# A decoder layer on one core: instruction orders, engine choices and PSUM banks laid out anew

## The chip, the cores and the metric

The kernel runs on one core of one Trainium2 chip, in one launch. The metric is the device time of that core in microseconds (us). Three runs of the kernel before took 178.32, 179.06 and 180.08 us; the median is 179.06 us.

## The reference

The layer has three parts on `x` (16 sequences of 128 tokens, 256 channels), each followed by a residual and a layer norm:

```python
x = layernorm(x + attention(x))          # 16 heads of 16 channels, 4 key/value heads, RMS norm, rope, causal
x = layernorm(x + wkv(x, ctx))           # channelwise recurrence over the 128 tokens, keys x, values ctx
x = layernorm(x + ffn(x))                # 256 -> 1024 -> 256, weights are signs, relu, per-channel scales
```

Attention: `q`, `k`, `v` by one projection with biases, `q` and `k` divided by their root mean square, rotated, `q` times a gain, causal softmax, and an output projection with bias. `wkv`: numerator and denominator of a weighted mean decay by `exp(-exp(time_decay))` at every token; the current token has the weight `exp(time_first)`. The feed-forward part: `relu(x @ sign(up).T) * up_scale`, then `@ sign(down).T * down_scale * output_scale`.

## The kernel before

The 16 sequences are worked on in 8 pairs `p` (`T = 2` sequences `t` in each). Every engine has one instruction stream, and all of them are written out by hand: small functions (`project`, `scores`, `exps`, `normed`, `low_bits`, ...) issue the instructions of one step of one pair, and a long list of calls at the end of each engine's block sets the order. Up to some seven pairs are under way at once, in different steps. Engines wait for each other by semaphores, one per step (`done(engine, step, p)`). A table `ON` says for the steps that several engines can do which engine does it for each pair (`V` VectorE, `G` GpSimd, which the profile calls POOL, `A` ScalarE). The eight PSUM banks are handed out by tables too (`PJ`, `SC`, `PV`, `AC`, `WO`, `X1`, `YT`, `X2`, `DN`, `UP`).

The steps of a pair, with the names used later:

- **project** (L417, L423): TensorE multiplies x by the weights in float32, then adds the biases by a matmul of ones with `bias_rows` (three bf16 rows that sum to the float32 bias, made by `split` on VectorE, L1518 to L1524, from a load of the biases into 96 partitions).
- **squares, head_sums, mean_log, first_root, newton_rms**: the root mean square of each head on ScalarE (square, logarithm, exponential) and VectorE; **rope_sines, rope_cosines, rope_sum** on VectorE; **scale_heads** gives `qn`; **high_heads, low_heads** split it in two float16 parts (`stack`), **swap_keys** writes the keys a second time the other way round. SyncE transposes `stack` to `rows` by DMA; for pair 0 TensorE does it (**first_rows**, L431) and ScalarE and VectorE copy the result out (L964, L1628).
- **scores** (L472, L479), **exps** (L971), **products** (L500), **attention_to_tokens**, **attend_norm**, **attention_to_channels**, **project_out** (L533), **residual** (0, the sum r1).
- layer norm n (0, 1 or 2): **moments(n, p)** on VectorE (L1676), **inverse_root** and **root** on POOL (L1355, L1361), then **normed(n, p)**, on VectorE (L1691) in two instructions that take the mean and the factor, or on ScalarE (L1035), which needs **offsets(n, p)** (L1682) from VectorE first.
- the recurrence: **keys**, **keys_by_context**, **scan** (L1702, VectorE, one instruction over numerator and denominator), **mix** (L1712), then the quotient by **log_den, first_rec, den_by_rec** (L1729, or L1395 on POOL)**, num_by_rec** (L1734, or L1400 on POOL)**, refine, add_mixed**.
- the feed-forward part in four quarters n: **high_x2, low_x2**, **ffn_up** (L576), **relu** (L1019), **high_bits** (L1025, float16 part), **low_bits** (L1760, the rest), **ffn_down** (L597), **scale_out** (L1766), **add_out** (L1773), layer norm 2, **store** by SyncE.

The code holds a second version of the attention scores for large gains (`row_scores`, `row_maxima`), which subtracts row maxima first. A flag computed on the chip from the gains chooses. TensorE reads it once (L612) and has two whole bodies, plain and guarded. VectorE reads it once and has eight short conditional blocks around `row_maxima(p)`. With these inputs the plain path runs.

## Time and profile before

| | |
|---|---|
| runs | 178.32, 179.06, 180.08 us |
| profiled execution, first to last instruction | 178.1 us (no time of its own is listed beside this span) |
| TensorE matmuls | 157.8 us busy, 89% of the span |
| VectorE | 156.5 us, 88% |
| ScalarE | 138.9 us, 78% |
| POOL | 83.4 us, 47% |
| mean granted TensorE clock | 0.979 |

The trace is of one execution. Busy shares are means over a beginning in which one pair is under way, a long middle in which several are, and an end in which only the last pair is left. What bounds each of them is to be read from its own stretch: which engine has hardly any idle time there, and, in the idle time of an engine, what ended it (`<-` and the name of the instruction that released it).

### The profile page before, as it was taken

To read this page: it belongs to the slowest core of one execution; us is meant where nothing else is said; L and a number is where in the kernel's file an instruction comes from. 1 tells how busy PE (TensorE), PEld (TensorE's weight loads), DVE (VectorE), ACT (ScalarE), POOL (GpSimd) and SP (SyncE) were. 2 spreads that over 40 slices of the span, in tenths; PEclk is the share of its full clock that TensorE was granted. 3 is DMA by queue.
4 is the path that set the end of the run, shared out by engine and by line. 5 is a ranking of instruction groups with operands and counts; after the bars stand their busy time and mean duration, and the time that the engine had idled before them with its cause. 6 is when DMAs were issued, how large, how long until landed. Compare 5 with 4: busy or idle time off the path is not lost.

```text
span 178.1 us, 3837 instructions
## 1 busy us (share of the span) xinstructions
PE 157.8 (89%) x1388; PEld 107.8 (61%) x1388; DVE 156.5 (88%) x289; ACT 138.9 (78%) x280; POOL 83.4 (47%) x109
## 2 busy tenths in 40 slices
PE   7978769989999999999999999999969798999920
PEld 2445424545645645566886668769758687898810
DVE  1489679798789999999899999999999999999981
ACT  3745488988998889999899989696687897898700
POOL 8282601017404695020873623699679457270121
PEclk9999969999999999999999999999999999999995
DMA  5899039044709107941070310000300010001122
GB/s 175 244 320 392 5 62 209 2 92 75 249 0 95 56 2 94 212 127 48 0 151 0 75 48 2 0 4 0 118 0 4 0 59 0 36 27 61 63 79 107
DMA packets 17989, 14.65 MB, mean 82 GB/s; under 512 B 12656, under 2 KB 13616, under 8 KB 17712
## 3 DMA queue, kind: packets, MB, share of 16 engines
q1 hardware_dynamic: 17424, 13.87, 29.8%
q10 hardware_dynamic: 544, 0.50, 0.9%
q8 instruction: 13, 0.21, 0.5%
q14 instruction: 8, 0.07, 0.1%
HBM read 9.52 MB, written 2.10 MB: 65 GB/s over the span
## 4 chain that ended last, share of the span: by engine, by line
PE 48%; DVE 27%; ACT 10%; issue 8%; DMA 3%; POOL 2%; SPq 0%; POOLq 0%; DVEq 0%; ACTq 0%
PE banks L417 9%; PE banks L576 8%; PE banks L500 7%; PE banks L597 6%; PE banks L533 5%; DVE hid_lo L1760 5%; DVE state L1702 4%; PE banks L472 4%; ACT probs L971 3%; DMA probs<-biases_dram 3%; DVE ratio L1712 2%; DVE stats L1676 2%; PE banks L510 2%; ACT dn_sb L918 2%; PE banks L479 2%
## 5 line engine op out<-in xcount | busy, mean ns | idle before, releaser
L971 ACT ACTIVATE probs<-banks 128x1024 f32<-128x1024 f32 x32 | 31.8, 1022 | 4.8 <-PE banks L479 4.8
L597 PE MATMUL banks<-dn_sb,hid_hi 128*128 128x256 bf16 x128 | 29.1, 272 | 1.1 <-DVE hid_lo L1760 1.1
L576 PE MATMUL banks<-x2hi,up_sb 128*128 128x256 f16 x128 | 29.1, 273 | 0.8 <-DVE x2lo L1753 0.5
L597 PE MATMUL banks<-dn_sb,hid_lo 128*128 128x256 bf16 x128 | 29.1, 273 | 0.0
L576 PE MATMUL banks<-x2lo,up_sb 128*128 128x256 f16 x128 | 29.0, 272 | 0.0
L417 PE MATMUL banks<-wqkv_sb,xT_sb 128*128 128x384 f32 x64 | 23.5, 512 | 2.0 <-issue 1.6
L1355 POOL TENSOR_SCALAR veps<-stats 128x2 f32<-128x2 f32 x24 | 9.4, 394 | 27.8 <-DVE stats L1676 26.8
L1361 POOL TENSOR_TENSOR rstd<-veps,half_neg 128x2 f32<-128x2 f32 x24 | 20.4, 853 | 1.3
L1019 ACT ACTIVATE banks<-banks,ups_man 128x256 f32<-128x256 f32 x48 | 19.6, 470 | 1.8 <-PE banks L576 1.6
L417 PEld LDWEIGHTS banks<-wqkv_sb,xT_sb 128*128 128x128 f32 x64 | 12.4, 201 | 11.9 <-issue 3.4
L1702 DVE TENSOR_TENSOR_SCAN state<-dec_sb,ke 128x1032 f32<-128x1032 f32 x8 | 18.4, 2301 | 0.0
L500 PE MATMUL banks<-probs,v_sb 128*32 128x512 f32 x128 | 17.6, 632 | 0.2
L576 PEld LDWEIGHTS banks<-x2hi,up_sb 128*128 128x128 f16 x128 | 12.5, 98 | 6.0 <-issue 3.8
L1760 DVE TENSOR_TENSOR hid_lo<-banks,hid_hi 128x512 f16<-128x512 f32 x24 | 16.0, 679 | 0.0
L1025 ACT ACTIVATE hid_hi<-banks 128x512 f16<-128x512 f32 x24 | 14.3, 616 | 1.7 <-PE banks L597 0.8
L533 PE MATMUL banks<-wo_sb,attT_sb 128*128 128x256 f32 x64 | 15.1, 379 | 0.0
L597 PEld LDWEIGHTS banks<-dn_sb,hid_hi 128*128 128x128 f16 x128 | 12.5, 98 | 3.4 <-issue 1.8
L597 PEld LDWEIGHTS banks<-dn_sb,hid_lo 128*128 128x128 f16 x128 | 12.5, 98 | 1.5
L576 PEld LDWEIGHTS banks<-x2lo,up_sb 128*128 128x128 f16 x128 | 12.5, 98 | 1.4
L533 PEld LDWEIGHTS banks<-wo_sb,attT_sb 128*128 128x128 f32 x64 | 12.2, 190 | 1.5
L472 PE MATMUL banks<-rows 32*128 32x512 f16 x128 | 10.2, 394 | 3.2 <-ACT probs L971 1.5
L1405 POOL TENSOR_TENSOR hid_lo<-hid,hid_hi 128x512 f16<-128x512 f32 x5 | 5.8, 1168 | 14.7 <-ACT hid_hi L1025 14.6
(129 smaller groups left out, 355.8 us busy)
## 6 DMA issues: line engine op xcount, KB each, us to landing
ctxT_sb<-ctxT_dram SPq DMA_DIRECT2D x8, 256.0 KB, 3.1
x_sb<-x_dram SPq DMA_DIRECT2D x8, 256.0 KB, 3.8
out_dram<-outb SPq DMA_DIRECT2D x8, 256.0 KB, 2.2
xT_sb<-xT_dram SPq DMA_DIRECT2D x7, 256.0 KB, 4.4
up_f<-up_dram SPq DMA_DIRECT2D x1, 1024.0 KB, 6.4
dn_f<-down_dram SPq DMA_DIRECT2D x1, 1024.0 KB, 8.4
wqkv_sb<-wqkv_dram ACTq DMA_DIRECT2D x2, 192.0 KB, 3.1
xT_sb<-xT_dram SPq DMA_DIRECT2D x2, 128.0 KB, 2.9
```

The source lines that it names most:

```text
L417: nc.tensor.matmul(banks[:, b + t, 0:E], xT_sb[:, p % XT_N, c, t, :], wqkv_sb[:, c, :], start=(c == 0), stop=False)
L472: nc.tensor.matmul(banks[:, b[g]], q[r:r + VW, kb, :], q[r:r + VW, HB * t:HB * t + REP, :].rearrange("p j s -> p (j s)"), start=(k == 0), ...
L500: nc.tensor.matmul(banks[r:r + VW, PV[p][t], :], v_sb[:, p % V_N, t, g, :], probs[:, (T * p + t) % PROBS_N, g].rearrange("p j s -> p (j s) ...
L533: mm = nc.tensor.matmul(banks[:, WO[p], t * D:(t + 1) * D], attT_sb[:, c, t, :], wo_sb[:, c, :], start=False, stop=(t == T - 1 and c == NC ...
L576: mm = nc.tensor.matmul(banks[:, UP[p][n], s * T * S:(s + 1) * T * S], up_sb[:, c, j * 128:(j + 1) * 128], part[:, c, :, :].rearrange("p t ...
L597: mm = nc.tensor.matmul(banks[:, DN[p], t * D:(t + 1) * D], part[:, t * S:(t + 1) * S], down_of(j), start=(j == 0 and t == 0 and m == 0), ...
L971: nc.scalar.activation(probs[:, (T * p + t) % PROBS_N, 2 * h:2 * h + 2].rearrange("p n j s -> p n (j s)"), banks[:, b:b + 2], ACT.Exp).the ...
L1019: nc.scalar.activation(hidden(p, n)[:, s], banks[:, UP[p][n], s * T * S:(s + 1) * T * S], ACT.Relu, scale=ups_man[:, j:j + 1]).then_inc(se ...
L1025: nc.scalar.activation(hid_hi[:, 2 * n:2 * n + 2], hidden(p, n), ACT.Copy)\
L1361: nc.gpsimd.tensor_tensor(rstd[n][:, p % MV_N], veps[n][:, p % MV_N], half_neg[:], ALU.pow)\
L1702: nc.vector.tensor_tensor_scan(state[:, 1:2 * W + 1], dec_sb[:].rearrange("p c a t s -> p (c a t s)"), ke[:, p % KE_N].rearrange("p c a t ...
L1760: nc.vector.tensor_tensor(hid_lo[:, 2 * n:2 * n + 2], hidden(p, n), hid_hi[:, 2 * n:2 * n + 2], ALU.subtract).then_inc(signal(f"lo{n}_done ...
```

## The change

What it does:

1. The lists of calls on all five engines are in another order, and the tables of banks hold other numbers.
2. `ON` has other engines: `low_heads` is always on POOL (before three of eight on VectorE), `swap_keys` four times on VectorE (before once), seven of 32 `high_bits` on POOL (before none), and more of the recurrence's products on POOL. `hid` in SBUF or PSUM is chosen by a table `HID`.
3. More norms on ScalarE: before `normed(1, p)` of all pairs; now `normed(0, p)` for pairs 5 and 6, `normed(1, p)` for 0 to 6 and `normed(2, p)` for 0, 1, 2, 5 and 6 (`NORM_ON_ACT`), with `offsets` on VectorE for each of them.
4. VectorE has one branch: after the flag there are two whole bodies, as on TensorE. TensorE reads the flag after `project(3)` and `first_rows`, no longer after `project(1)`.
5. The biases are loaded into three partitions (0, 32, 64) in one DMA, into a buffer (`outb`) that VectorE clears first; before, they went into 96 partitions in two DMAs. The output bias is split on VectorE, before on POOL. The load of the gains moves from ScalarE's queue to SyncE's.
6. The last pair's end is divided by sequence: the last quarter of `ffn_down(7)` by halves, `scale_half` and `add_half` instead of `scale_out` and `add_out`, and two stores of half the size.

TensorE, from `project(1)` to the first scores (xT_sb: the tokens by channel; flags: the branch). Before:

```order
L417 MATMUL banks<-wqkv_sb,xT_sb 128x384 x4
L423 MATMUL banks<-bias_rows,ones_b 128x384 x2
L612 TENSOR_LOAD flags
L612 ISA x2
L869 COMPARE_AND_BRANCH
L417 MATMUL banks<-wqkv_sb,xT_sb 128x384 x4
L423 MATMUL banks<-bias_rows,ones_b 128x384 x2
L417 MATMUL banks<-wqkv_sb,xT_sb 128x384 x4
L423 MATMUL banks<-bias_rows,ones_b 128x384 x2
L431 MATMUL banks<-id_h,stack 128x128 x12
L472 MATMUL banks<-rows 128x512 x8
```

Now:

```order
L434 MATMUL banks<-wqkv_sb,xT_sb 128x384 x4
L440 MATMUL banks<-bias_rows,ones_b 128x384 x2
L434 MATMUL banks<-wqkv_sb,xT_sb 128x384 x4
L440 MATMUL banks<-bias_rows,ones_b 128x384 x2
L434 MATMUL banks<-wqkv_sb,xT_sb 128x384 x4
L440 MATMUL banks<-bias_rows,ones_b 128x384 x2
L448 MATMUL banks<-id_h,stack 128x128 x12
L648 TENSOR_LOAD flags
L648 ISA x2
L883 COMPARE_AND_BRANCH
L495 MATMUL banks<-rows 128x512 x8
```

Two projections and the transposition of pair 0 stand ahead of the read of the flag, which stands right ahead of the first scores.

VectorE's last instructions (r: the sum before norm 2; outb: what is stored). Before:

```order
L1760 TENSOR_TENSOR hid_lo<-banks,hid_hi 128x512
L1691 TENSOR_SCALAR outb<-r,stats,rstd 128x256 x2
L1676 BN_STATS stats<-r 128x6
L1766 TENSOR_TENSOR banks<-banks,dsc_b 128x512
L1773 TENSOR_TENSOR r<-banks,x 128x512
L1691 TENSOR_SCALAR outb<-r,stats,rstd 128x256 x2
L1676 BN_STATS stats<-r 128x6
L1691 TENSOR_SCALAR outb<-r,stats,rstd 128x256 x2
```

Now:

```order
L1751 TENSOR_TENSOR hid_lo<-banks,hid_hi 128x512
L1757 TENSOR_TENSOR r<-banks,dsc_b 128x512
L1670 SCALAR_TENSOR_TENSOR offset<-stats,rstd 128x2
L1751 TENSOR_TENSOR hid_lo<-banks,hid_hi 128x512
L1664 BN_STATS stats<-r 128x6
L1770 TENSOR_TENSOR banks<-banks,dsc_b 128x256
L1775 TENSOR_TENSOR r<-banks,x 128x256
L1770 TENSOR_TENSOR banks<-banks,dsc_b 128x256
L1775 TENSOR_TENSOR r<-banks,x 128x256
L1664 BN_STATS stats<-r 128x6
L1670 SCALAR_TENSOR_TENSOR offset<-stats,rstd 128x2
L1679 TENSOR_SCALAR outb<-r,stats,rstd 128x256 x2
```

The scaling and the addition of the last pair are four instructions of half the size, and `normed(2, 6)`, which stood between the addition and the last moments, is gone to ScalarE (its offset is left, after the last moments).

POOL, from `keys_by_context(6)` on. Before:

```order
L1389 TENSOR_TENSOR ke<-ke,ctxT_sb 128x2x2x128
L1355 TENSOR_SCALAR veps1<-stats1 128x2
L1361 TENSOR_TENSOR rstd1<-veps1,half_neg 128x2
L1389 TENSOR_TENSOR ke<-ke,ctxT_sb 128x2x2x128
L1400 TENSOR_TENSOR ratio<-ratio,rec0 128x2x256
L1405 TENSOR_TENSOR hid_lo<-hid,hid_hi 128x512
L1411 TENSOR_TENSOR r3<-r3,x2 128x512
L1355 TENSOR_SCALAR veps1<-stats1 128x2
L1361 TENSOR_TENSOR rstd1<-veps1,half_neg 128x2
```

Now:

```order
L1371 TENSOR_TENSOR ke<-ke,ctxT_sb 128x2x2x128 x2
L1343 TENSOR_TENSOR rstd2<-veps2,half_neg 128x2
L1382 TENSOR_TENSOR ratio<-ratio,rec0 128x2x256
L1377 TENSOR_TENSOR newt<-ratio,rec0 128x512
L1392 TENSOR_TENSOR hid_lo<-hid,hid_hi 128x512
L1387 CAST hid_hi<-hid 128x512
L1337 TENSOR_SCALAR veps1<-stats1 128x2
L1343 TENSOR_TENSOR rstd1<-veps1,half_neg 128x2
L1387 CAST hid_hi<-hid 128x512
L1392 TENSOR_TENSOR hid_lo<-hid,hid_hi 128x512
```

The addition is gone from here to VectorE, and both products of pair 6 and three parts `hid_hi` of later pairs have come or moved up.

The diff, cut (function bodies that only change names, and the lists of calls, are left out but for a few lines):

```diff
         ON = dict(
-            qn_done="GGVVGGGV",
-            hi_done="AGGGGAGA",
-            lo_done="VGVVGGGG",
-            stack_done="AVAAAAAA",
-            kv_done="VGVVGVGG",
-            newt_done="GGGVGGVG",
-            guess_done="VVVGGVGV",
-            lo2_done="GGGVGGVV",
-            r3_done="GGVGVVVV")
+            guess_done="GVVGGVGV",
+            hi0_done="GGAGAGAA",
+            hi2_done="AGAAAGGA",
+            hi_done="AGAGGGAA",
+            kv_done="VGGVGVGG",
+            lo1_done="VVGVVVVV",
+            lo2_done="GVVVVVVV",
+            lo3_done="VVGVGGVV",
+            newt_done="GGGGGGGV",
+            out_done="AAAVVAAV",
+            qn_done="VGVGVGGV",
+            r3_done="GVVVVVGV",
+            stack_done="AAVVVAVA",
+            x1_done="VVVVVAAV",
+            x2_done="AAAAAAAV")
+        NORM_ON_ACT = ((0, 0, 0, 0, 0, 1, 1, 0), (1, 1, 1, 1, 1, 1, 1, 0), (1, 1, 1, 0, 0, 1, 1, 0))
...
-            sp.dma_start(bias_in[:, 0:E], biases[0:E].partition_broadcast(BR)).then_inc(bias_in_done, 16)
+            sp.wait_ge(bias_clear, 1)
+            sp.dma_start(bias_in[0:BR:32], biases.partition_broadcast(3)).then_inc(bias_in_done, 16)
+            for dst, src in gain_loads:
+                sp.dma_start(dst, src).then_inc(gains_in, 16)
...
-            store(7)
+            store_half(7, 0)
+            store_half(7, 1)
...
             project(0)
             project(1)
-            pe.wait_ge(masks_ready, MASKS)
-            pe.wait_ge(guard_ready, GUARDS)
+            project(2)
+            done(pe, "rot_done", 0)
+            project(3)
+            first_rows()
             pe.wait_ge(gain_ready, GAINS)
             plain = pe.value_load(flags[0:1, 0:1], min_val=0, max_val=1)
...
+            def ffn_down_half(p, t):
+                n = NJ // 2 - 1
+                hidden_there(p, n)
+                for s in range(2):
+                    j = 2 * n + s
+                    for m, part in enumerate((hid_hi, hid_lo)):
+                        mm = nc.tensor.matmul(down_tile(p, t), part[:, j, t * S:(t + 1) * S], dn_sb[:, j],
+                                              start=False, stop=(s == 1 and m == 1))
+                mm.then_inc(sems["dn_mm"], 1)
...
+            def high_bits(p, n):
+                done(pool, "hid_done", p, 2 * n + 2)
+                nc.gpsimd.tensor_copy(hid_hi[:, 2 * n:2 * n + 2], hidden(p, n)).then_inc(signal(f"hi{n}_done", p), 1)
...
+            nc.vector.memset(bias_in, 0.0).then_inc(bias_clear, 1)
...
-            with dve.If(guarded):
-                row_maxima(0)
...
+            def scale_half(p, t):
+                done(dve, "dn_mm", p, NJ // 2 + t)
+                nc.vector.tensor_tensor(down_tile(p, t), down_tile(p, t), dsc_b[:], ALU.mult).then_inc(sems["o3_done"], 1)
+            def add_half(p, t):
+                done(dve, "o3_done", p, t + 1)
+                nc.vector.tensor_tensor(r3[:, p % R3_N, t], down_tile(p, t), x2[:, p % X2_N, t], ALU.add)\
+                    .then_inc(signal("r3_done", p), 1)
...
+            with dve.If(plain):
+                from_heads(False)
+            with dve.Else():
+                from_heads(True)
```

## Rows read from the trace of the kernel before

**Rows 1.** The page, part 1: busy us (share of the span), xinstructions.
```profile
PE 157.8 (89%) x1388; PEld 107.8 (61%) x1388; DVE 156.5 (88%) x289; ACT 138.9 (78%) x280; POOL 83.4 (47%) x109
```

**Rows 2.** Windows: us, busy PE, PEld, DVE, ACT, POOL (x); granted clock, DMA share, GB/s.
```profile
110.00:150.00 40.00, 36.38 (x319) 29.94 (x317) 39.84 (x65) 31.63 (x68) 28.34 (x28) 1.00 0.06 20
160.00:170.00 10.00, 10.00 (x94) 8.81 (x93) 9.13 (x18) 7.69 (x17) 1.17 (x3) 1.00 0.15 56
```

**Rows 3.** Timeline from 0 to 22 us: start us, busy us, engine, line, operation, idle before.
```profile
4.68 3.88 PE L417 MATMUL banks<-wqkv_sb,xT_sb 128*128 128x384 f32 x8
...
8.92 0.50 PE L423 MATMUL banks<-bias_rows,ones_b 96*128 96x384 bf16 x2 [0.35 <-DVE bias_rows L1524]
...
12.20 0.61 POOL L1338 CAST maskq_sb<-probs 128x512 bf16<-128x512 f32 x1
...
13.92 2.84 PE L417 MATMUL banks<-wqkv_sb,xT_sb 128*128 128x384 f32 x8 [1.59 <-issue]
...
17.88 0.51 ACT L957 ACTIVATE stack<-stack 128x128 f16<-128x128 f16 x2
...
19.83 0.83 PE L431 MATMUL banks<-id_h,stack 128*128 128x128 f16 x12
...
21.78 0.40 PE L472 MATMUL banks<-rows 32*128 32x512 f16 x4 [1.12 <-ACT rows L964]
```

**Rows 4.** Timeline from 22 to 26 us, VectorE and TensorE.
```profile
22.30 0.83 DVE L1612 TENSOR_TENSOR banks<-banks,cos_sb 128x640 f32<-128x640 f32 x1 [0.45 <-issue]
...
24.10 1.04 PE L472 MATMUL banks<-rows 32*128 32x512 f16 x8 [1.48 <-ACT probs L971]
```

**Rows 5.** Windows of 24 to 27 us and of 29 to 31 us.
```profile
24.00:27.00 3.00, 2.90 (x32) 0.93 (x32) 1.98 (x6) 2.23 (x5) 0.00 (x0) 0.51 0.94 97
29.00:31.00 2.00, 2.00 (x19) 0.85 (x21) 1.91 (x7) 1.35 (x3) 0.72 (x1) 1.00 0.79 288
```

**Rows 6.** Groups by line and shape: xcount | busy us, mean ns | idle before.
```profile
L1035 ACT ACTIVATE x<-z,offset,rstd 128x256 f32<-128x256 f32 x16 | 8.8, 613 | 1.3 <-DVE offset L1682 1.2
L1395 POOL TENSOR_TENSOR newt<-ratio,rec 128x512 f32<-128x512 f32 x6 | 7.6, 1268 | 7.9 <-ACT rec L1004 7.8
...
L1381 POOL TENSOR_TENSOR stack<-qn,stack 128x640 f16<-128x640 f32 x5 | 7.0, 1402 | 0.4 <-ACT stack L948 0.2
...
L1691 DVE TENSOR_SCALAR outb<-r,stats,rstd 128x256 f32<-128x256 f32 x16 | 5.8, 404 | 1.2 <-POOL rstd L1361 1.2
...
L1642 DVE TENSOR_TENSOR stack<-qn,stack 128x640 f16<-128x640 f32 x3 | 2.5, 822 | 0.2
...
L1682 DVE SCALAR_TENSOR_TENSOR offset<-stats,rstd 128x2 f32<-128x2 f32 x8 | 1.5, 190 | 0.0
...
L1338 POOL CAST maskq_sb<-probs 128x512 bf16<-128x512 f32 x1 | 0.6, 613 | 0.1
```

**Rows 7.** Timeline from 138 to 144 us: a scan on VectorE and a product on POOL.
```profile
139.83 2.29 DVE L1702 TENSOR_TENSOR_SCAN state<-dec_sb,ke 128x1032 f32<-128x1032 f32 x1
...
140.71 2.48 POOL L1400 TENSOR_TENSOR ratio<-ratio,rec 128x512 f32<-128x512 f32 x1 [2.74 <-ACT rec L1004]
```

**Rows 8.** Timeline of the end, from 170 us, VectorE and POOL.
```profile
170.49 0.70 DVE L1766 TENSOR_TENSOR banks<-banks,dsc_b 128x512 f32<-128x512 f32 x1
...
172.54 0.69 DVE L1676 BATCH_NORM_STATS2 stats<-r 128x6 f32<-128x512 f32 x1
...
173.67 0.69 POOL L1361 TENSOR_TENSOR rstd<-veps,half_neg 128x2 f32<-128x2 f32 x1
174.47 0.73 DVE L1691 TENSOR_SCALAR outb<-r,stats,rstd 128x256 f32<-128x256 f32 x2 [1.23 <-POOL rstd L1361]
```

**Rows 9.** Waits of SyncE's queue: us in total, times, longest us.
```profile
SPq L284 <- DMA out_dram<-outb: 2.1, 1, 2.1
```

**Rows 10.** DMA issues: tile, queue, count, KB each, median us from issue to landing.
```profile
xT_sb<-xT_dram SPq DMA_DIRECT2D x2, 128.0 KB, 2.9
...
probs<-biases_dram SPq DMA_DIRECT2D x1, 144.0 KB, 5.3
```

More of the change, by code:

```diff
@@ L614, in from_scores @@
             def from_scores(guarded):
-                project(2)
-                done(pe, "rot_done", 0)
-                project(3)
-                done(pe, "rot_done", 1)
-                first_rows()
                 if guarded:
@@ L1752, in low_x2 @@
                 done(dve, "x2hi_done", p)
[L1753 to L1755 removed]
+                if X2_BY_DMA[p]:
+                    high, low = [x2h[:, p % X2H_N, part].rearrange("p t c d -> p (t c d)") for part in range(2)]
+                    whole = x2[:, p % X2_N].rearrange("p t d -> p (t d)")
+                else:
+                    high, low, whole = x2_part(p, 0), x2_part(p, 1), banks[:, X2[p]]
+                nc.vector.tensor_tensor(low, whole, high, ALU.subtract).then_inc(signal("x2lo_done", p), 1)
             def low_bits(p, n):
@@ L1827, in _ @@
-            done(dve, "rscale_done", 4)
-            head_sums(5)
-            rope_sines(5)
-            attend_norm(1)
-            rope_cosines(5)
-            normed(0, 0)
-            rope_sum(5)
-            newton_rms(5)
-            keys_by_context(0)
-            scan(0)
-            residual(1)
-            mix(0)
-            with dve.If(guarded):
-                row_maxima(3)
-            moments(0, 1)
-            rope_sines(6)
-            rope_cosines(6)
-            attend_norm(2)
@@ L1863, in _ @@
-            offsets(1, 0)
-            rope_cosines(7)
-            rope_sum(7)
-            scan(1)
-            with dve.If(guarded):
-                row_maxima(5)
-            residual(3)
-            mix(1)
-            low_x2(0)
-            newton_rms(7)
-            keys_by_context(2)
-            attend_norm(4)
-            moments(0, 3)
-            num_by_rec(1)
-            scale_heads(7)
-            scan(2)
-            refine(1)
-            low_bits(0, 0)
-            done(dve, "ny_done", 1)
@@ L1901, in _ @@
-            done(dve, "x1_done", 3)
-            residual(5)
-            with dve.If(guarded):
-                row_maxima(7)
-            low_x2(1)
-            keys_by_context(3)
-            offsets(1, 2)
-            scan(3)
-            moments(0, 5)
-            moments(2, 0)
-            mix(3)
-            low_bits(1, 0)
-            done(dve, "ratio_done", 3)
-            scan(4)
-            low_x2(2)
-            attend_norm(6)
-            low_bits(1, 1)
-            den_by_rec(3)
```

1074 lines of the change are left out of this document (548 added, 526 removed).

## The prediction

> **What bounds the kernel now.** I read the page's busy line first, then the windows, then the two ends in the timeline. The busy line [rows 1] has TensorE and VectorE nearly level at 89 and 88% of 178.1 us, so no single engine is the bound, and the stretches must say it. The windows [rows 2] say it: from 110 to 150 us VectorE is busy for 39.8 of 40 us, while TensorE is idle for 3.6 us of them, ScalarE for 8.4 and POOL for 11.7. From 160 to 170 us the order is turned round: TensorE is full, VectorE has 9.13. So the middle waits for VectorE, and the last pairs for TensorE.
>
> The beginning is a chain of short waits, each of which the reader finds in the bracket of a row. TensorE's first projection runs from 4.68 to 8.56 us, and its bias matmul waits for the bias rows until 8.92, a wait of 0.35 [rows 3]. After project(1) TensorE stands for 1.59 us, "issue": it has the table of masks to wait for, whose last cast on POOL ends at 12.81 (12.20 + 0.61), and then reads the flag and branches, another 1.1 us until 13.92 [rows 3]. Pair 0's heads are ready in `stack` at 18.39 (17.88 + 0.51), but TensorE only comes to them behind project(3), at 19.83. It then waits 1.12 us for ScalarE's copy of the rows, and the first scores start at 21.78. The next scores wait 1.48 us and start at 24.10 [rows 4], and from 24 to 27 us the granted clock is 0.51, the lower of TensorE's two levels, 1.2 GHz [rows 5].
>
> The end is one chain on VectorE and POOL after TensorE's last matmul: the scale starts at 170.49, then come the addition and a norm of pair 6, the moments at 172.54, the root on POOL at 173.67, the norm from 174.47 to 175.20 [rows 8], and then the store, for which SyncE waits 2.1 us [rows 9].
>
> **The beginning: -2.0 us.** The load of the biases (144 KB in 96 rows) takes 5.3 us to land; the first tokens, issued just before, take 2.9 [rows 10]. Three rows in place of 96 land between these two, sooner by up to 2.4 us, or not at all sooner if they queue behind the same traffic. It hardly matters: project(0) itself ends at 8.56, so at most 0.35 us comes of it [rows 3]. The clearing of the buffer is a memset on an idle VectorE while SyncE issues the tokens, cost nothing; if SyncE had to wait for it, the slack of the bias covers some tenths. The load of the gains, moved in front of the rope tables and all later loads on SyncE, delays these by one issue, under half a microsecond, and none was waited for.
>
> TensorE then runs projects 1, 2 and 3 without a stop. Project(1) ended 1.59 us ahead of 13.92, at 12.33, and now ends at 12.0; projects 2 and 3 took from 13.92 to 19.83, so project(3) ends at 12.0 + 5.9 = 17.9 [rows 3]. The stack of pair 0 must be ready by then. In the new order its scaling is on VectorE (0.8 instead of 1.3 us, by the nearest rows), its low part on POOL (1.40 instead of 0.82, [rows 6]); the two cancel, and what is left are ScalarE's earlier start by 0.35 and a key swap with less ahead of it, which puts the stack at about 17.6 to 18.0. So first_rows starts at 17.9 against 19.83, 2.0 us earlier. The read of the flag now stands behind it: 1.1 us, and it lies beside ScalarE's copy of the rows, in which TensorE stood for 1.12 us anyway [rows 3]; without that cover it would cost its 1.1. The first scores start at 19.7 and the second at about 22.1, where the rotation of pair 2 on VectorE and the first exponentials come out together. The fall of the clock has the same two waits ahead of it, so I leave it in. On TensorE the same work lies between there and project(5) in both orders. Bounds: 0.35 us (the stack is late and nothing moves) and 2.0 + 1.5, when the clock doesn't fall (3 us at half speed, [rows 5]).
>
> **One branch on VectorE: 0.** The eight conditional blocks look costly and are not: the first, with the read of the flag, leaves 0.45 us of issue [rows 4], and of the two microseconds from 29 to 31 us, in which the second one stands, VectorE is busy for 1.91 [rows 5]. The read now stands ahead of head_sums(0), where VectorE has to wait for the first squares. There are 0 to 0.5 + 7 x 0.09 = 1.1 us to have, if every idle time is the branch's; VectorE did not bound that part, so I take 0.
>
> VectorE must now jump over the guarded body at its end. The row that bears on it is SyncE's wait of 2.1 us for the last store [rows 9], which starts as VectorE is done and covers a jump of up to that length; the sum has 0 for it. The Trainium skill, "Runtime: NRT & Kernel Launch", section "Instruction fetch mechanics", speaks against this change: a taken branch to a target outside the fetched window forces a fetch before execution goes on. By that rule the end would still be hidden as long as the fetch is shorter than the store, and no row here shows VectorE making such a jump.
>
> **The middle: -2.0 us.** VectorE's work falls. Norms: 12 halves less at 0.404 (-4.8), low heads three less at 0.82 (-2.5), offsets six more at 0.19 (+1.1) [rows 6]. The other moves are products and additions of 0.7 to 0.8 us, three away and two come, key swaps, and the output bias with four small instructions: together about +1.7. The sum is -4.5 of 156.5 us. From 110 to 150 us alone it is ten halves less (norm 0 of pairs 5 and 6, norm 2 of pairs 0, 1 and 2), -4.0, and five offsets, +0.95; two products leave and two additions come. That is -3.1 us where VectorE has no idle time. It can pay out only until TensorE is full, and TensorE's idle time there is 3.6 us. ScalarE gets twelve halves more, at 0.613 each 7.4 us in all, and gives back seven `hid_hi` and six short copies [rows 6]; it has the 8.4 us of idle time in this stretch to take them. I take 2.0 of the 3.1, since each norm on ScalarE adds an offset and a turn in another queue to its chain, and POOL's products are slower. Bounds: 0, and 3.6.
>
> POOL gets three low heads at 1.40, seven casts of 128x512 at 0.6 (the nearest is the mask's, [rows 6]) and three products at about 1.3, and gives away some. That is +7 us on an engine with 53% idle time, so in sum free, but not in latency. The row to see is POOL's product at 140.71: it takes 2.48 us, where its like takes 1.27, because VectorE's scan runs from 139.83 to 142.12 [rows 6, 7]. The Trainium skill, "SBUF — State Buffer", section "Who interferes with whom", says that a VectorE instruction with two SBUF inputs and a GpSimd instruction that reads SBUF lock each other out for a whole instruction. The row agrees: the product ends 1.07 us after the scan. By the rule each of the 13 added POOL instructions may be stretched so; this is the third rival below.
>
> **The end: -0.9 us.** Scaling the first sequence starts under TensorE's last matmuls. After the last one, half a scale and half an addition are left, about 0.8 if each half of a 0.70 costs 0.4, and the norm of pair 6 is gone. So the moments start 0.8 to 0.9 us after the last matmul and not 172.54 - 170.49 = 2.05 [rows 8]: -1.2. Against it, the last store is two issues, the second issued about 0.4 later than one alone would be (a norm half is 0.404, [rows 6], and the first issue takes about as long): +0.3. Bounds: 0, if the halves cost as much as wholes, and -1.3.
>
> **Sum.** -2.0 - 2.0 - 0.9 = -4.9, with nothing between 30 and 110 us, where both engines are nearly full. 178.1 - 4.9 = 173.2 us of span. The median of the runs is 0.9 us above this execution's span, so I forecast a median of 174.1, 2.8% less.
>
> **Rivals.**
> - *The middle gives nothing* (17%): the chain from VectorE to POOL to ScalarE and back is as long as the work taken off VectorE. For it: ScalarE waited for an offset already in the trace (1.2 us in [rows 6]). Against: the full VectorE windows. 174.1 + 2.0 = 176.1.
> - *More than that* (12%): the clock doesn't fall at 24 us, or TensorE's idle time in the middle vanishes. 174.1 - 1.6 = 172.5. For it: the beginning has one stop of 1.6 us less. Against: the two waits right ahead of the fall stay [rows 3, 4].
> - *Slower* (9%): POOL's longer list is held up by VectorE's scans and products, on the way to the heads and to ffn_down, which waits for `hid_hi` and then `hid_lo`. Each hold costs 1.2 us (2.48 less 1.27, [rows 6, 7]). All 13 added instructions on the path would cost 15.6, half of them 7.8: 174.1 + 7.8 = 181.9. It turns the gain of 4.9 when more than four of the 13 are on the path. Against it: POOL is idle for 11.7 of the 40 us in which the lists are longest [rows 2].
> - *No change* (12%): four such holds, or the order of one engine wrong in one place (a load behind a wait on SyncE's queue: ctx of pair 6 now stands behind store(0), before ahead of it). 179.
> - The forecast's own case has 50%, from 172.8 to 175.5.
>
> A difference of 1% (1.8 us) is what a measurement can tell from no change. Faster by over 1% are the forecast, the first two rivals and little else: 0.78. Within 1%: 0.13. Slower: 0.09. The range of 8 in 10 leaves out the slower case and the outer tail of the best: 171.5 to 177.8.
>
> **What would show it.** First scores near 19.7 us and first_rows near 17.9; no issue gap after project(1); a gap of about 1.1 us ahead of the first scores. TensorE busy for over 38 of the 40 us in the middle, ScalarE for over 36. A fall of the granted clock near 22 us, as before at 24. From TensorE's last matmul to the last moments' start 0.9 us. It is wrong if POOL's casts take over 1 us each, if TensorE waits for `hid_hi` on POOL, or if VectorE's windows stay at 9.9 with the same end: then the work was put elsewhere on it.

## The result, and the profile after

The changed kernel takes 182.60 us (median of four runs, 182.25 to 183.03), the kernel before, measured beside it, 178.69 (177.56 to 180.08): a ratio of 1.0205, 95% interval 1.0146 to 1.0264. It is slower by 3.9 us; 174.1 was forecast.

The busy line of the page after, against [rows 1]:

```profile
PE 156.7 (87%) x1388; PEld 107.3 (59%) x1388; DVE 161.2 (89%) x291; ACT 141.4 (78%) x280; POOL 91.4 (51%) x115
```

VectorE was to fall from 156.5 to 152.0 us and rose to 161.2. The timeline of the beginning (start, busy, engine, line) answers to [rows 3, 4], and the window to [rows 5]:

```profile
17.37 0.84 PE L448 MATMUL banks<-id_h,stack 128*128 128x128 f16 x12
...
19.33 0.61 PE L495 MATMUL banks<-rows 32*128 32x512 f16 x8 [1.12 <-ACT rows L975]
...
22.08 0.61 PE L495 MATMUL banks<-rows 32*128 32x512 f16 x8 [1.92 <-DVE rot L1614]
```

```profile
24.00:27.00 3.00, 3.00 (x20) 1.29 (x22) 2.96 (x6) 2.52 (x7) 0.00 (x0) 1.00 0.85 189
```

The beginning came as forecast and a little better: first_rows starts 2.5 us sooner and the first scores at 19.33 (19.7 forecast). The fall of the clock at 24 us, which the forecast left in, is gone: the granted clock is 1.00 from 24 to 27 us, where it was 0.51. The first matmul of scores(1) starts at 27.80, before at 30.50. Then the lead is lost. From there to the first matmul of ffn_up(1) it is 66.8 us before and 71.0 now, and from that one to the last instruction 80.8 before and 81.75 now. In the middle [rows 2], TensorE's idle time fell as hoped, from 3.6 to 2.4 us of 40, and VectorE is as full as it was:

```profile
110.00:120.00 10.00, 9.39 (x92) 7.46 (x89) 9.97 (x17) 7.54 (x15) 4.81 (x6) 1.00 0.01 2
120.00:130.00 10.00, 9.88 (x80) 7.68 (x79) 9.97 (x18) 8.67 (x19) 6.94 (x9) 1.00 0.00 0
130.00:140.00 10.00, 9.09 (x79) 7.41 (x76) 9.91 (x18) 9.67 (x24) 7.71 (x11) 1.00 0.22 80
140.00:150.00 10.00, 9.27 (x84) 8.19 (x85) 9.97 (x16) 9.57 (x23) 5.20 (x6) 1.00 0.07 27
```

Where VectorE's time went shows when groups are kept apart by shape (count | busy us, mean ns | idle before):

```profile
L1751 DVE TENSOR_TENSOR hid_lo<-banks,hid_hi 128x512 f16<-128x512 f32 x19 | 12.6, 680 | 0.1
L1679 DVE TENSOR_SCALAR x<-r,stats,rstd 128x256 f32<-128x256 f32 x12 | 7.5, 668 | 0.0
L1751 DVE TENSOR_TENSOR hid_lo<-hid,hid_hi 128x512 f16<-128x512 f32 x8 | 7.0, 870 | 0.1
L1630 DVE TENSOR_TENSOR qn<-rot,rscale 128x640 f32<-128x640 f32 x4 | 4.2, 1061 | 0.1
```

A norm half takes 404 ns in [rows 6] and 668 here on average; a subtraction from SBUF 870, the same one from PSUM 680; a scaling of the heads 1061 where 820 is usual. Most instructions of a group have their usual length and a few are 0.3 to 1.2 us longer. VectorE and POOL in the timeline show when:

```profile
27.32 0.20 DVE L1585 TENSOR_TENSOR rscale<-ny,gain_b 128x40 f32<-128x40 f32 x1
...
27.60 1.28 POOL L1350 TENSOR_TENSOR qn<-rot,rscale 128x640 f32<-128x640 f32 x1 [5.47 <-DVE rscale L1585]
27.65 1.38 DVE L1550 TENSOR_SCALAR dsc_b<-dsc_b,osc_b 128x256 f32<-128x256 f32 x1
28.95 0.72 POOL L1356 CAST stack<-qn 128x640 f16<-128x640 f32 x1
29.06 0.62 DVE L1552 TENSOR_SCALAR u_rest<-u_clip 128x2 f32<-128x2 f32 x1
29.62 1.40 POOL L1363 TENSOR_TENSOR stack<-qn,stack 128x640 f16<-128x640 f32 x1
29.72 1.33 DVE L1554 TENSOR_SCALAR k_bias<-u_rest 128x2 f32<-128x2 f32 x1
...
62.51 0.69 POOL L1343 TENSOR_TENSOR rstd<-veps,half_neg 128x2 f32<-128x2 f32 x1
63.02 1.82 DVE L1679 TENSOR_SCALAR x<-r,stats,rstd 128x256 f32<-128x256 f32 x2
63.16 1.53 POOL L1363 TENSOR_TENSOR stack<-qn,stack 128x640 f16<-128x640 f32 x1
```

An instruction on two elements per partition (`k_bias`, 128x2) takes 1.33 us: it started 0.10 us after a POOL instruction and ended with it, at 31.05 and 31.02. The two norm halves at 63.02 take 1.82 us in place of 0.72 and end at 64.84, POOL's `low_heads` at 64.69. Laid beside POOL's, 14 of VectorE's instructions in this trace are too long by 10.6 us in all, each overlapping a POOL instruction that reads SBUF. In the trace before there are four, 2.3 us. No reduction, no batch statistics and no instruction with an operand in PSUM is among them, though such instructions often start inside a POOL read too: 35 products, sums and differences with a PSUM operand do so in the trace after, and none of them is longer by over 0.03 us. An instruction that is too long in this way is called held below, and the time too much a hold.

### The profile page after: what moved, and what is told of

Read it like the earlier page. It is cut to its first block, busy times and chain, and to the rows that moved or that the text cites. A ratio compares the mean times of both kernels' runs of the same rounds, so it can differ in the third digit from the quotient of the medians.

```text
span 180.5 us, 3809 instructions
## 1 busy us (share of the span) xinstructions
PE 156.7 (87%) x1388; PEld 107.3 (59%) x1388; DVE 161.2 (89%) x291; ACT 141.4 (78%) x280; POOL 91.4 (51%) x115
## 4 chain that ended last, share of the span: by engine, by line
DVE 55%; PE 19%; issue 11%; ACT 10%; POOL 2%; POOLq 0%; DVEq 0%; ACTq 0%
DVE state L1690 9%; DVE hid_lo L1751 6%; PE banks L434 5%; DVE stats L1664 5%; DVE ratio L1700 4%; PE banks L600 4%; ACT probs L982 3%; DVE banks L1607 3%; DVE rope_b L1600 3%; DVE rot L1614 3%; PE banks L621 2%; DVE ssum L1570 2%; DVE x2T L1746 2%; DVE z L1735 2%; PE banks L639 2%
## 5 line engine op out<-in xcount | busy, mean ns | idle before, releaser
L600 PE MATMUL banks<-x2T,up_sb 128*128 128x256 f16 x256 | 32.3, 273 | 1.8 <-DVE x2T L1746 1.7
L621 PE MATMUL banks<-dn_sb,hid_hi 128*128 128x256 bf16 x124 | 28.5, 273 | 0.8 <-DVE hid_lo L1751 0.6
L621 PE MATMUL banks<-dn_sb,hid_lo 128*128 128x256 bf16 x124 | 28.5, 273 | 0.0
L600 PEld LDWEIGHTS banks<-x2T,up_sb 128*128 128x128 f16 x256 | 24.3, 98 | 6.8 <-DVE x2T L1746 3.0
L1343 POOL TENSOR_TENSOR rstd<-veps,half_neg 128x2 f32<-128x2 f32 x24 | 18.2, 758 | 1.5
L1035 ACT ACTIVATE banks<-banks,ups_man 128x256 f32<-128x256 f32 x38 | 15.7, 461 | 3.8 <-PE banks L600 3.7
L523 PE MATMUL banks<-probs,v_sb 128*32 128x512 f32 x128 | 16.6, 603 | 0.0
L1363 POOL TENSOR_TENSOR stack<-qn,stack 128x640 f16<-128x640 f32 x8 | 11.7, 1472 | 8.2 <-ACT stack L959 8.1
L1751 DVE TENSOR_TENSOR hid_lo<-banks,hid_hi 128x512 f16<-128x512 f32 x19 | 12.6, 680 | 0.1
L1700 DVE SCALAR_TENSOR_TENSOR ratio<-ke,now_gain,state 128x512 f32<-128x512 f32 x16 | 12.7, 832 | 0.0
L1377 POOL TENSOR_TENSOR newt<-ratio,rec 128x512 f32<-128x512 f32 x7 | 10.2, 1451 | 3.8 <-ACT rec L1015 3.7
L1664 DVE BATCH_NORM_STATS2 stats<-r 128x6 f32<-128x512 f32 x16 | 11.1, 697 | 0.9 <-POOL r L1398 0.7
```

The source lines that it names most:

```text
L523: nc.tensor.matmul(banks[r:r + VW, PV[p][t], :], v_sb[:, p % V_N, t, g, :], probs[:, (T * p + t) % PROBS_N, g].rearrange("p j s -> p (j s) ...
L600: mm = nc.tensor.matmul(banks[:, UP[p][n], s * T * S:(s + 1) * T * S] .rearrange("p (t s) -> p t s", t=T), up_sb[:, c, j * 128:(j + 1) * 1 ...
L621: mm = nc.tensor.matmul(down_tile(p, t), part[:, j, t * S:(t + 1) * S], dn_sb[:, j], start=(j == 0 and m == 0 and (t == 0 or p == PAIRS - 1)),
L1035: nc.scalar.activation(hidden(p, n)[:, s], banks[:, UP[p][n], s * T * S:(s + 1) * T * S], ACT.Relu, scale=ups_man[:, j:j + 1]).then_inc(se ...
L1343: nc.gpsimd.tensor_tensor(rstd[n][:, p % MV_N], veps[n][:, p % MV_N], half_neg[:], ALU.pow)\
L1664: nc.vector.bn_stats(stats[n][:, p % MV_N].rearrange("p t k -> p (t k)"), rows_of.rearrange("p t d -> p d t"))\
```

## The experiments

**Theory 1, the holds:** a VectorE instruction that starts inside a POOL instruction reading SBUF waits until that one ends. **Theory 2, the order:** the new lists and POOL's longer latency cost the time, and the stretched instructions lie in slack. Each ratio is to the runs of the kernel before in the same batch (their medians 178.8 to 179.2); differences between two changed kernels are differences of their medians.

### Holds taken out of the changed kernel

`e1_const` moves one call on VectorE, in both bodies:

```diff
+                small_constants()
                 rope_sines(3)
                 newton_rms(2)
...
                 newton_rms(3)
-                small_constants()
```

> The changed kernel with one edit: VectorE's six small constants stand ahead of rope_sines(3), where POOL has nothing to do, and not behind newton_rms(3), which releases POOL's scale_heads(3). Theory (a VectorE instruction that starts inside a POOL instruction that reads SBUF waits until that one ends): the three constants that took 1.38, 0.62 and 1.33 us take 0.35, 0.17 and 0.17, VectorE's busy time falls by about 2.6 us, head_sums(4) starts near 28.5 instead of 30.96, and the whole is 1.0 to 2.5 us faster than the changed kernel (about 180 to 181.5 where that has 182.6). Rival 1 (the time was lost in the order of the lists and in POOL's latency, the stretched constants lie in slack): the constants are short, but the whole stays within 0.5 us of the changed kernel. Rival 2 (the constants are slow in themselves): they stay at 1.4, 0.6 and 1.3.

180.96 us, ratio to before 1.0106 [1.0023, 1.0189]: 1.6 us faster than the change. The intervals of the two ratios overlap, the runs do not (180.63 to 181.48 here, 182.25 to 183.03 there). The same two constants in its timeline:

```profile
21.66 0.35 DVE L1550 TENSOR_SCALAR dsc_b<-dsc_b,osc_b 128x256 f32<-128x256 f32 x1
...
22.25 0.17 DVE L1554 TENSOR_SCALAR k_bias<-u_rest 128x2 f32<-128x2 f32 x1
```

They aren't slow in themselves (rival 2 falls), and they weren't in slack (rival 1 falls). head_sums(4) starts at 29.53, not 28.5: it waits for ScalarE's squares, so part of the 2.6 us met the next wait.

`e2_waits` adds waits on POOL and nothing else:

```diff
+            done(pool, "x1_done", 1)
             low_heads(5)
...
+            done(pool, "x1_done", 2)
             low_heads(6)
...
+            done(pool, "x1_done", 4)
             add_out(0)
```

> The changed kernel with three waits added on POOL and nothing else: low_heads(5) waits until VectorE's normed(0, 1) is done, low_heads(6) until normed(0, 2) is, add_out(0) until normed(0, 4) is. Theory (VectorE held by POOL's reads): the three norm halves of 1.50, 1.50 and 1.36 us become 0.40 each, VectorE's busy time falls by 3.1 us and the whole by 1.5 to 3, though POOL only gets more to wait for. Rival (POOL's latency is what costs): the whole stays, or becomes 0.5 to 2 us slower, since POOL's three instructions start up to 0.7 us later.

180.51 us, 1.0115 [1.0082, 1.0148]: 2.1 us faster, by waiting more. POOL starts after the norm, which is short again:

```profile
61.97 0.69 POOL L1343 TENSOR_TENSOR rstd<-veps,half_neg 128x2 f32<-128x2 f32 x1
62.48 0.73 DVE L1682 TENSOR_SCALAR x<-r,stats,rstd 128x256 f32<-128x256 f32 x2
63.29 1.41 POOL L1363 TENSOR_TENSOR stack<-qn,stack 128x640 f16<-128x640 f32 x1 [0.63 <-DVE x L1682]
```

By theory 2 more waiting on POOL could only have cost time. `e5_fix` has both edits and three more: two waits on POOL, and den_by_rec(1) goes from POOL to VectorE:

```diff
-            newt_done="GGGGGGGV",
+            newt_done="GVGGGGGV",
...
+            done(pool, "qn_done", 7)
             low_bits(0, 2)
...
+            done(pool, "ratio_done", 4)
             low_bits(2, 1)
```

> The changed kernel with the edits of e1_const and e2_waits together and three more: on POOL low_bits(0, 2) waits for VectorE's scale_heads(7) and low_bits(2, 1) for mix(4), and den_by_rec(1) is on VectorE. Theory (the time was lost to VectorE instructions that POOL's reads hold up, and the losses add): VectorE's busy time falls from 161.2 to about 153.5 us, the stretched norms, scale_heads(7) and mix(4) are gone, and the whole is near 177.7 us (176.5 to 179), below the kernel before. Rival (only what is lost ahead of 70 us counts, from then on TensorE or ScalarE bound it): near 180, as e2_waits.

178.46 us, 0.9968 [0.9928, 1.0009]: 4.1 us of the change's time are gone, the losses add. VectorE is busy for 155.2 us; 3.3 of them are holds that are left (a copy at 40 us, a mix at 82, four more from 96 to 105). Without them it would be 151.9. The other direction, VectorE holding POOL, stayed as it was: those of POOL's instructions that take over 0.25 us more than usual are too long by 10.1 us in all in the kernel before, 11.1 in the change and 11.0 in `e5_fix`.

`e6_writes` puts memsets, which read nothing, in the place of POOL's large products, sums, differences and casts. What these steps compute is left out; order and waits stay. For example in `low_bits`:

```diff
-                nc.gpsimd.tensor_tensor(hid_lo[:, 2 * n:2 * n + 2], hidden(p, n),
-                                        hid_hi[:, 2 * n:2 * n + 2], ALU.subtract).then_inc(signal(f"lo{n}_done", p), 1)
+                nc.gpsimd.memset(hid_lo[:, 2 * n:2 * n + 2], 0.0).then_inc(waste, 1)
+                wasted()
+                nc.gpsimd.memset(hid_lo[:, 2 * n:2 * n + 2], 0.0).then_inc(signal(f"lo{n}_done", p), 1)
```

> The changed kernel with all of POOL's products, sums, splits and casts of 128x512 and 128x640 replaced by memsets of their outputs, two or three in a row so that POOL is busy for about as long (1.0 to 1.4 us each); what these steps compute is left out, order, waits and semaphores stay. Theory (POOL's reading of SBUF holds VectorE, writing alone does not): no VectorE instruction is stretched any more, its busy time falls from 161.2 to about 151 us, and the whole is 173 to 177 us. Rival 1 (POOL's mere activity or its latency costs the time): stretches and the whole stay, 180 or more. Rival 2 (other things bind once VectorE is free): no stretches, yet 178 or more.

177.26 us, 0.9913 [0.9873, 0.9954]: 5.3 us less than the change, a little outside the range expected. The groups again:

```profile
L1703 DVE TENSOR_SCALAR x<-r,stats,rstd 128x256 f32<-128x256 f32 x12 | 6.9, 616 | 0.0
L1775 DVE TENSOR_TENSOR hid_lo<-hid,hid_hi 128x512 f16<-128x512 f32 x8 | 5.4, 679 | 0.1
L1654 DVE TENSOR_TENSOR qn<-rot,rscale 128x640 f32<-128x640 f32 x4 | 3.3, 820 | 0.1
```

Products and differences are at their normal 679 and 820 ns. The norms are not (616): beside memsets six halves took 0.69 to 0.95 us, and so did four of the small constants by `tensor_scalar` (0.39 to 0.75). So VectorE was busy for 155.1 us, not for the 151 expected. "Writing does not hold VectorE" was too wide: it holds the norm, not the product of two operands.

### Holds put into the kernel before

Those runs moved POOL's timing too. `e13_reads` adds seven products to `e3_head` (below) in POOL's idle time; `e14_memsets` has three memsets in the place of each:

```diff
+            def extra(name, p, k=None):
+                done(pool, name, p, k)
...
+                nc.gpsimd.tensor_tensor(scratch[:], up_f[:, 0, 0:512], up_f[:, 1, 0:512], ALU.mult).then_inc(waste, 1)
...
             keys_by_context(1)
+            extra("r1_done", 3)
             den_by_rec(1)
+            extra("guess_done", 1)
+            extra("scan_done", 2)
             low_bits(0, 2)
```

> The kernel of e3_head with seven extra products on POOL, two SBUF operands of 128x512 each, into a scratch buffer, at seven places where POOL is idle for at least 1.5 us and VectorE works without a pause (after residual(3), num_by_rec(1), scan(2), den_by_rec(3), low_bits(2, 0), the first mix(6) and num_by_rec(7)). None of POOL's own instructions has to start later. Theory (POOL's reads hold VectorE): four to seven VectorE instructions are stretched by 0.4 to 1.2 us, VectorE's busy time rises by 4 to 7 us, and the whole is 2 to 5 us slower than e3_head's 176.6. Rival (the holds only happened where VectorE had slack, or come from POOL's real work): the whole within 0.7 us of e3_head.

> As e13_reads, but each of the seven extra products is three memsets of the scratch buffer, about 1.3 us of POOL in all, which read nothing. Theory (it is the reading): no VectorE instruction with two SBUF operands is stretched, norms in halves by 0.4 us at most, and the whole is within 0.7 us of e3_head. Rival (any POOL instruction holds VectorE): as slow as e13_reads.

184.40 us, 1.0341 [1.0298, 1.0384], with reads; 177.18 us, 0.9936 [0.9904, 0.9969], with memsets. The first place, with reads:

```profile
70.71 2.42 DVE L1730 SCALAR_TENSOR_TENSOR ratio<-ke,now_gain,state 128x512 f32<-128x512 f32 x2
70.88 1.71 POOL L1422 TENSOR_TENSOR scratch<-up_f 128x512 f32<-128x512 f32 x1 [3.22 <-DVE r L1687]
```

with memsets:

```profile
70.89 1.41 DVE L1731 SCALAR_TENSOR_TENSOR ratio<-ke,now_gain,state 128x512 f32<-128x512 f32 x2
71.04 1.48 POOL L1423 MEMSET scratch<- 128x512 f32 x3 [3.21 <-DVE r L1688]
```

and the busy lines, reads first:

```profile
PE 158.8 (87%) x1388; PEld 108.5 (59%) x1388; DVE 164.5 (90%) x289; ACT 139.1 (76%) x280; POOL 94.2 (52%) x116
```

```profile
PE 156.0 (89%) x1388; PEld 107.3 (61%) x1388; DVE 156.6 (90%) x289; ACT 138.8 (79%) x280; POOL 92.4 (53%) x130
```

Seven products raise VectorE's busy time by 7.9 us and the whole by 7.2 against memsets in the same places. Two thirds of it are direct: six VectorE instructions overlap one of the products and are held by 5.7 us in all. Three more are held for 2.8 us by POOL's own reads, which by the delay come to lie beside other instructions than with memsets. The granted clock is 0.83 from 140 to 150 us in the profile with reads and 1.00 with memsets, but it carries little: two of the four executions with reads have mean clocks of 0.984 and 0.985, as high as with memsets, and are as slow as the others. This shows the cause without any call of the layer in another place, and a price: what VectorE lost in the full stretches, the kernel lost nearly one for one. In `e5_fix` it was less, 4.1 us for 6.0 of VectorE's. The first place shows both directions: the first half of `mix` holds the product (1.71 in place of 1.27), then the product holds the second half. The Trainium skill, "SBUF — State Buffer", section "Who interferes with whom", states this: whoever issues first has the shared ports for its whole instruction, and the other fully blocks; a VectorE instruction with two SBUF inputs contends with a GpSimd instruction that reads SBUF and not with one that only writes, and copies, casts and `tensor_scalar` can enter modes that contend with GpSimd. The traces agree: the two halves of mix took 2.42 us beside a read and 1.41 beside memsets, norms are longer beside reads (1.50 in the change) and beside memsets (up to 0.95 in `e6_writes`), PSUM operands and reductions beside neither.

### The other parts

`e3_head`, the kernel before with TensorE's new beginning alone:

```diff
             project(1)
+            project(2)
+            done(pe, "rot_done", 0)
+            project(3)
+            done(pe, "rot_done", 1)
+            first_rows()
             pe.wait_ge(masks_ready, MASKS)
```

> The kernel before with the changed kernel's beginning on TensorE alone: project(2), project(3) and first_rows stand ahead of the read of the flag and its waits. Theory (this term of the prediction was right, -2.0 us): first_rows starts near 18.3 and the first scores near 20.3 instead of 21.78, and the whole is 1 to 2 us faster than before. Rival: the next wait, for the rotation of pair 2 on VectorE or for the exponentials, takes the place, and the whole moves by less than 0.5 us.

176.62 us, 0.9874 [0.9793, 0.9954]: 2.35 us faster. About 0.9 of it may be the clock's. The granted clock is 1.00 from 24 to 27 us here, and against those ten of the batch's 19 executions of the kernel before whose mean clock is 0.987 or more (median 178.0), the gain is 1.4 us.

```profile
17.12 0.83 PE L431 MATMUL banks<-id_h,stack 128*128 128x128 f16 x12
19.11 0.61 PE L472 MATMUL banks<-rows 32*128 32x512 f16 x8 [1.16 <-DVE rows L1628]
```

`e8_low` adds to it three `low_heads` on POOL:

```diff
-            lo_done="VGVVGGGG",
+            lo_done="GGGGGGGG",
```

> The kernel of e3_head with low_heads of pairs 0, 2 and 3 on POOL, as the change has them (three instructions of 0.82 us off VectorE, 1.40 us each on POOL). By the prediction this gives VectorE 2.5 us, of which the whole keeps 0 to 1 (175.6 to 176.6). By the theory that POOL's reads hold VectorE, each of the three may stretch one VectorE instruction by up to 1.2 us, and with the longer chain to the first scores the whole is 0 to 2 us slower (176.6 to 178.6).

177.62 us, 0.9952 [0.9901, 1.0002]: 1.0 us slower than `e3_head`, though 2.5 us of VectorE's work are gone. The rows of pair 0 come later (first scores at 19.86, `e3_head` 19.11), and four instructions of VectorE are held that were not: three small ones by 0.3, 0.4 and 0.8 us, and the constant `dsc_b`, which starts with a `low_heads` at 27.54, by 1.2. That is 2.7 us, as much as was taken off.

`e7_norms` puts five norms of the middle on ScalarE in `e3_head`, `e12_outnorms` only the three whose result is stored; per norm:

```diff
-            normed(2, 0)            (VectorE's list)
+            offsets(2, 0)
...
+            normed(2, 0)            (ScalarE's list)
```

> The kernel of e3_head (before, with the new beginning) with five more layer norms on ScalarE, as the change has them in the middle: normed(0, 5), normed(0, 6), normed(2, 0), normed(2, 1), normed(2, 2), with offsets on VectorE in their places. The prediction's middle term: VectorE has 4.0 us less in halves and 0.95 more in offsets, and the whole falls by up to 2 us from e3_head's 176.6 (174.6 to 175.6). Rival (a norm by ScalarE lengthens its chain, and ScalarE is full where it is put): no change, or up to 2 us slower.

> The kernel of e3_head with only the norms whose result is just stored on ScalarE: normed(2, 0), normed(2, 1), normed(2, 2). e7_norms, with normed(0, 5) and normed(0, 6) as well, was 5.6 us slower than e3_head. If it is the turn VectorE, ScalarE, TensorE on the path of x1 that costs, this one is near e3_head (176 to 177.5); if every added norm on ScalarE holds up its queue, it is 2 to 4 us slower (178.6 to 180.6).

182.23 us, 1.0171 [1.0074, 1.0267], and 179.27 us, 1.0014 [0.9963, 1.0064]: 5.6 and 2.65 us slower than `e3_head`. In `e7_norms` VectorE is no longer full from 110 to 150 us (34.9 us of 40, `e3_head` 39.6), TensorE even less (33.8, `e3_head` 36.1), and ScalarE's waits name the turn (us in total, times, longest):

```profile
ACT x L1040 <- DVE offset L1693: 3.9, 3, 2.0
```

`e7_norms` came out slower than either expectation. `e12_outnorms` lies where it was expected if every added norm on ScalarE holds up its queue, and leaves 3.0 us for the two norms on the path of x1: both paths cost. But one must not read it as the term's sign. `e10_normback` does the reverse in `e5_fix`: the five norms are back on VectorE, their calls moved from ScalarE's list to VectorE's, and the tables say so:

```diff
-        NORM_ON_ACT = ((0, 0, 0, 0, 0, 1, 1, 0), (1, 1, 1, 1, 1, 1, 1, 0), (1, 1, 1, 0, 0, 1, 1, 0))
+        NORM_ON_ACT = ((0, 0, 0, 0, 0, 0, 0, 0), (1, 1, 1, 1, 1, 1, 1, 0), (0, 0, 0, 0, 0, 1, 1, 0))
```

> The kernel of e5_fix with the five norms of the middle back on VectorE: normed(0, 5), normed(0, 6), normed(2, 0), normed(2, 1), normed(2, 2). By the prediction's middle term they give VectorE 3 us of work where it is full, and the whole is 1.5 to 2.5 us slower than e5_fix's 178.5 (180 to 181). Rival (what VectorE was relieved of came back as waits for offsets and for ScalarE): within 0.7 us of e5_fix, or faster.

185.19 us, 1.0319 [1.0230, 1.0408]: 6.7 us slower than `e5_fix`, over three times what was expected. VectorE is busy for 5.0 us more, and 2.1 of them are three new holds (norm halves at 125 and 147 us, a mix at 148). TensorE stops more, and the granted clock falls behind it, where `e5_fix` has 1.00 from 110 to 150 us:

```profile
120.00:130.00 10.00, 7.64 (x58) 6.24 (x56) 9.97 (x19) 5.51 (x12) 5.71 (x8) 1.00 0.23 79
130.00:140.00 10.00, 9.73 (x73) 8.21 (x72) 8.85 (x14) 8.38 (x20) 6.42 (x8) 0.83 0.01 2
```

Either order of calls is slower with the other's engines for these five norms. So neither run prices the norms by themselves; it is order and engines together that the change moved.

The end. `e4_end` gives the kernel before the halves, with normed(2, 6) behind the last moments:

```diff
-            scale_out(7)
+            scale_half(7, 0)
             done(dve, "out_done", 5)
-            add_out(7)
+            add_half(7, 0)
+            scale_half(7, 1)
+            add_half(7, 1)
+            moments(2, 7)
             landed(dve, "stored", 4)
             normed(2, 6)
-            moments(2, 7)
```

> The kernel before with the changed kernel's end alone: the last quarter of ffn_down(7), the scale and the addition by sequence, two stores of half the size, and normed(2, 6) behind moments(2, 7) instead of ahead of it. Theory (this term was right, -0.9 us): the last moments start about 0.9 us after TensorE's last matmul instead of 2.05 after the start of the scale, and the whole is 0.7 to 1.4 us faster than before. Rival: the halves cost as much as wholes and the second store adds a latency; the whole stays within 0.3 us.

179.28 us, 1.0019 [0.9966, 1.0071]: nothing that the runs can show. VectorE comes to the first half late, and four halves take nearly as long as two wholes and a norm (1.78 us to the moments, 2.05 in [rows 8]):

```profile
169.45 0.27 PE L622 MATMUL banks<-dn_sb,hid_lo 128*128 128x256 bf16 x1
169.72 0.42 DVE L1803 TENSOR_TENSOR banks<-banks,dsc_b 128x256 f32<-128x256 f32 x1
...
171.50 0.70 DVE L1700 BATCH_NORM_STATS2 stats<-r 128x6 f32<-128x512 f32 x1
```

The first half starts as TensorE's last matmul ends, not under it. `e11_addout` takes away, in `e5_fix`, VectorE's wait for POOL's add_out(6): VectorE does the addition itself (`r3_done="GVVVVVVV"`):

> The kernel of e5_fix with add_out(6) on VectorE, not on POOL. In the changed kernel VectorE waits 0.72 us for it, right ahead of the last pair's halves. Theory (this wait ate most of the end's gain): the last moments start 0.6 to 0.7 us earlier against the last matmul, and the whole is 0.3 to 0.7 us faster than e5_fix (near 178.0). Rival (VectorE gets 0.6 us more work, which takes the wait's place): no change.

178.68 us, 1.0003 [0.9962, 1.0044]: no change, and the last moments start 1.78 us after the last matmul (`e5_fix` 1.86); the rival was right. `e9_best` is `e3_head` with the halves, normed(2, 5) and normed(2, 6) on ScalarE and a wait on POOL at two holds, as in `e2_waits`; `e15_end2` leaves these two waits out.

> The kernel of e3_head with two holds taken off VectorE (POOL's den_by_rec(0) waits for num_by_rec(0), POOL's add_out(0) for normed(0, 4)), the end by halves of e4_end, and normed(2, 5) and normed(2, 6) on ScalarE, which is idle there. Theory: 1.05 and 0.8 us of VectorE's time come back ahead of 95 us, and the last moments start about 0.9 us earlier against the last matmul than in e3_head; 174.5 to 175.8 us where e3_head has 176.6. Rival (VectorE's time does not bind there, the halves give nothing as in e4_end): 176.6.

> The kernel of e9_best without its two waits on POOL: the new beginning and the end by halves with normed(2, 5) and normed(2, 6) on ScalarE. In e9_best the last moments started 1.40 us after the end of TensorE's last matmul, in e3_head 2.10, yet its time was the same. If the two waits cost what the end gave, this is 0.5 to 0.8 us faster than e3_head (175.8 to 176.1); if not, it is 176.5.

176.48 us, 0.9853 [0.9782, 0.9923], and 176.98 us, 0.9906 [0.9876, 0.9936]. The last moments start 1.40 us after the last matmul in place of 2.10, and the whole does not show it against `e3_head`. Both holds were only exchanged: den_by_rec(0), made to wait, then held newton_rms by 0.98 us, and a keys_by_context held an offset at 66.4 us by 0.94. VectorE's holds are 2.2 us in all, as in `e3_head`. These two and `e3_head` beat both kernels, the one before by 1.9 to 2.7 us and the change by 5.6 to 6.1; among themselves they can't be told apart.

## Why the prediction was wrong

- **Beginning, -2.0:** right in mechanism and sign. It is -2.35 alone and -2.7 at scores(1) in the change. "So I leave it in", of the clock's fall at 24 us, was not right: the profiles of the change and of `e3_head` have none there. Without the clock the gain is nearer to 1.4 (`e3_head` against executions of the kernel before at the same mean clock), so that the figure of 2.0 comes so close is in part luck. In the kernel before, 23 runs of one batch have spans of 175.8 to 176.9 us at a mean granted clock of 0.986 to 0.991, or of 177.0 to 180.2 at 0.982 and less; the profile shown before (178.1 at 0.979) was one of the latter.
- **One branch on VectorE, 0:** nothing in the traces speaks against it; it was not tried alone.
- **Middle, -2.0: this is the step that failed.** Its count of VectorE's work was near: without the holds the kernel before has 154.2 us (156.5 less 2.3) and the change 150.6 (161.2 less 10.6), 3.6 less, where 4.5 was forecast. (That `e5_fix` has 151.9 without holds and the forecast 152.0 is chance: the forecast's 156.5 had 2.3 us of holds in it.) What failed is "The sum is -4.5 of 156.5 us" as VectorE's time: it took only the instructions that were moved and gave each its duration from [rows 6]. An instruction's duration on VectorE depends on what POOL does beside it; the sum came out at +4.7.
- **The third rival** had the mechanism and the time (181.9, 182.6 measured), the wrong way round and at 9%. I quoted that the two "lock each other out" and then priced one direction: VectorE holding POOL, "on an engine with 53% idle time". The direction that counts is POOL holding VectorE, since VectorE is full. The rows for it were in the same trace: four of VectorE's instructions too long, 2.3 us. The direction that was priced hardly moved (POOL too long by 10.1 us before, 11.1 in the change), so the nearness of 181.9 is luck.
- **What the middle gave apart from holds:** from scores(1) to ffn_up(1) 66.8 us before, 71.0 in the change, 66.5 in `e5_fix`, 66.1 in `e6_writes`; from there to the end 80.8, 81.75, 80.95 and 79.9. So holds cost 4.5 to 4.9 us in the first stretch and 0.8 to 1.8 in the second. What is left of the middle and the end together, in this second stretch, is between +0.2 and -0.9, not -2.9. "The middle gives nothing" (17%) was right on this part.
- **End, -0.9:** wrong. "Scaling the first sequence starts under TensorE's last matmuls" assumed a VectorE with nothing else to do; it is late itself. In the change it also waited 0.72 us for add_out(6), on POOL by the new table, which I had not followed up: the last moments start at 174.24, 1.86 us after the last matmul. Taking this wait away gained nothing either (`e11_addout`).

The ledger in medians: beginning -2.35, holds +4.1 (those removed in `e5_fix`) to +5.3 (`e6_writes`), end 0. With +3.9 in all, +0.95 to +2.15 is left. I can't name it. `low_heads` on POOL cost 1.0 us in `e8_low`, but that run brought 2.7 us of holds of its own, so it can't be set beside the term for holds. What stays open too: the time outside the span is 2.2 to 2.5 us in the change and 1.8 to 1.9 before; `e14_memsets`, with no edit of the branch, has 2.2 as well, `e11_addout` 1.5, so it isn't shown to be VectorE's jump.

## What to carry to other kernels

Before moving work to POOL, list which VectorE instructions will start inside its reads: every product, cast or sum on POOL is a lock for VectorE's products, scans, copies and norms with operands in SBUF (not for reductions, batch statistics or operands in PSUM), and if VectorE is full it costs up to the POOL instruction's whole length. The typical clash is built in by one event that releases both engines (a root that VectorE's norm and POOL's next call follow); three waits on the idle engine, without any less work, gave back 2.1 us. Such a wait can also only pass the hold on to the next instruction, as in `e9_best`, so look at the new trace. And price a change in order and engines at one or two places by editing just these: a sum of durations can't see what one engine's timing does to another's.

## What the hardware showed that I had not expected

- Being small doesn't protect the one who waits: instructions on 128x2 took 1.33 and 0.62 us beside POOL's reads, 0.17 without. The one on 128x1 that lies inside a POOL read in the change (`flags`, 7.37 us) was not held; what tells it from the others no run shows.
- Holds repeat to a hundredth of a microsecond: the same three instructions (at 80, 84 and 113 us in the change) are held by the same 1.02, 0.97 and 0.99 us in the change, `e1_const` and `e2_waits`.
- A late VectorE can cost more than its lateness: in `e10_normback` TensorE was busy for 7.64 of the 10 us from 120 to 130, and the granted clock is 0.83 in the next window and again from 150 to 160 us, that is the lower level, 1.2 GHz, for a third of each. VectorE was busy for 5.0 us more than in `e5_fix`, the whole took 6.7 more. How much of it is the clock's is open.
